# A transformer block with routed experts: experts' rows added by accumulating scatters, every shared chunk ahead of the experts

## The reference

```python
mod = (silu(c) @ wmod).reshape(4, 6, 1, 512)            # sa, ca, ga, sb, cb, gb per batch
ga, gb = sign(ga) * max(|ga|, 0.25), sign(gb) * max(|gb|, 0.25)
h = layernorm(x) * (1 + ca) + sa
x = x + ga * attention(h)        # 16 heads of 32, relu(q), relu(k); vk = [v;1] k^T per head and batch
                                 # out = vk q, divided by its last row, then @ w_proj.T + b_proj
h = layernorm(x) * (1 + cb) + sb
gate = top-2 of 8 experts by sigmoid(h @ gate_w.T) + router_bias, weights normalized
y = sum over the two experts e of gate_e * (silu(h W1[e]) * (h W3[e])) W2[e]     # 352 wide
s = (silu(h sw1) * (h sw3)) sw2                                                  # shared, 704 wide
out = x + gb * (y + s)
```

## Time and profile before

| what | us |
|---|---|
| three runs | 1329.02, 1335.45, 1338.58 (median 1335.45) |
| the profiled execution's own time | 1328.03 |
| its span | 1326.3 |
| PE busy in the span | 1229.3 (93%) |
| DVE, ACT, POOL busy | 664.9, 413.8, 396.9 |
| mean granted clock | 0.976 |

### The profile page before, as it was taken

The page is one execution under the profiler, slowest core; times in us unless marked ns, Lnnn a source line. Parts: engine busy times, 40 slices in busy tenths (PEclk is TensorE's granted clock), DMA queues, the critical chain, the costliest instruction groups (busy, mean ns, idle before and its releaser), DMA issues.

```text
span 1326.3 us, 25206 instructions
## 1 busy us (share of the span) xinstructions
PE 1229.3 (93%) x9054; PEld 781.5 (59%) x9054; DVE 664.9 (50%) x1382; ACT 413.8 (31%) x869; POOL 396.9 (30%) x367
## 2 busy tenths in 40 slices
PE   6998998998997998977896999999999999989998
PEld 2645665665565665654564565656656665657675
DVE  6455877867777666577884211111111111126465
ACT  4332444433443332423333122222222222212121
POOL 2112656655654433200001011111111111056552
PEclk9998999999999999988998999999999999989999
DMA  7714687898896865733444455555565565489986
GB/s 233 210 42 128 165 192 191 197 219 167 206 214 162 235 184 166 233 124 112 139 146 129 112 130 133 142 123 141 135 129 137 128 141 130 111 224 239 253 232 173
DMA packets 269204, 219.08 MB, mean 165 GB/s; under 512 B 188496, under 2 KB 200784, under 8 KB 268572
## 3 DMA queue, kind: packets, MB, share of 16 engines
q1 hardware_dynamic: 239832, 155.31, 45.7%
q0 software_dynamic: 12848, 35.40, 12.0%
q10 hardware_dynamic: 16408, 26.77, 6.4%
HBM read 116.69 MB, written 56.94 MB: 131 GB/s over the span
## 4 chain that ended last, share of the span: by engine, by line
PE 51%; DVE 15%; POOL 10%; DMA 10%; issue 8%; ACT 3%; SPq 2%; ACTq 1%; DVEq 0%; POOLq 0%
PE ps_o L86 6%; PE ps_o L88 6%; PE ps_o L87 6%; PE ps_vs L86 5%; PE ps_vs L87 5%; PE ps_vs L88 5%; DMA xt<-g 3%; DMA wp_raw<-in_wproj_t 2%; PE ps_vh L86 2%; PE ps_vh L88 2%; PE ps_vh L87 2%; POOL ol L412 2%; DVE w_all L682 2%; POOL h L388 2%; POOL h L399 2%
## 5 line engine op out<-in xcount | busy, mean ns | idle before, releaser
L471 POOL DMA_INDIRECT g<-h_d,slot_token x71 | 67.8, 956 | 507.1 <-DMA xt<-g 350.0
L86 PE MATMUL ps_o<-w_all,xt 128*128 x568 | 178.7, 315 | 11.6 <-DMA xt<-g 11.6
L88 PE MATMUL ps_o<-w_all,xt 128*128 x568 | 178.6, 315 | 0.0
L87 PE MATMUL ps_o<-w_all,xt 128*128 x568 | 178.6, 314 | 0.0
L914 DVE TENSOR_TENSOR at<-ps_y,at 128x384 f16<-128x384 f32 x71 | 39.6, 558 | 176.5 <-ACT at L1171 176.5
L909 DVE SCALAR_TENSOR_TENSOR a<-ps_o,a 128x352 f32<-128x352 f32 x71 | 37.3, 525 | 173.1 <-PE ps_o L88 173.1
L1176 ACT ACTIVATE y<-ps_vs,slot_weight 128x512 f32<-128x512 f32 x71 | 48.8, 688 | 230.6 <-PE ps_vs L88 230.6
L86 PE MATMUL ps_qh<-ht,wqkv 128*128 128x128 f16 x512 | 88.9, 221 | 8.3 <-DVE qt L549 4.9
L88 PE MATMUL ps_qh<-ht,wqkv 128*128 128x128 f16 x512 | 88.9, 221 | 0.0
L87 PE MATMUL ps_qh<-ht,wqkv 128*128 128x128 f16 x512 | 88.9, 221 | 0.0
L86 PE MATMUL ps_kh<-s_ht,sh 128*128 128x256 f16 x256 | 71.3, 278 | 12.4 <-DMA s_ht<-h2t_d 8.9
(11 more groups left out here) (240 smaller groups left out, 3179.6 us busy)
## 6 DMA issues: line engine op xcount, KB each, us to landing
y_d<-y SPq DMA_DIRECT2D x71, 256.0 KB, 3.5
w_stage<-in_w_d ACTq DMA_DIRECT2D x64, 176.0 KB, 2.5
xb<-in_x SPq DMA_DIRECT2D x32, 256.0 KB, 3.5
xr<-in_x SPq DMA_DIRECT2D x32, 256.0 KB, 3.7
x_d<-x SPq DMA_DIRECT2D x32, 256.0 KB, 3.4
h_d<-hl SPq DMA_DIRECT2D x32, 256.0 KB, 2.6
h2t_d<-h2t SPq DMA_DIRECT2D x32, 256.0 KB, 3.4
s_xs<-x_d SPq DMA_DIRECT2D x32, 256.0 KB
```

The lines of the kernel that those rows point to most:

```text
L86: nc.tensor.matmul(out, lh, rh, start=first, stop=False, skip_group_check=True)
L87: nc.tensor.matmul(out, lh, rl, start=False, stop=False, skip_group_check=True)
L88: return nc.tensor.matmul(out, ll, rh, start=False, stop=last, skip_group_check=True)
L471: pool.indirect_dma_start(m.g[:, t % 2, :], None, m.h2_d, bass.IndirectOffsetOnAxis(ap=m.slot_token[:, t:t + 1], axis=0)).then_inc(m.gathe ...
```

## The change

Diff, cut to its core:

```diff
-LAG = BT
+LAG = BT + 1
-EARLY = 9
-EARLY_STEPS = SH_TILES * EARLY
+EARLY_STEPS = SH_TILES * CHUNKS
-X_RING, QT_RING, ... Y_RING, YB = 4, 9, 3, 2, 3, 3, 6, 4, 4, 8
+X_RING, QT_RING, ... W_RING = 4, 10, 3, 2, 3, 3, 6, 4
+G_RING, GB_RING, Y_RING = 4, 3, 3
-TURNS_PER_STEP = 2
-TURNS_FROM = TAIL_STEPS + 7
+TURNS_FROM = TAIL_STEPS + 11
-LAST_PIECES = 4
+LAST_PIECES = 6
 def w_turn(q):
     if q < TAIL_STEPS:
-        return range(q, q + 1)
-    if q <= LIST_STEP:
-        return spread(TAIL_STEPS, SHARED_PIECES, q - TAIL_STEPS, LIST_STEP + 1 - TAIL_STEPS)
+        return range(q // 2, q // 2 + 1) if q % 2 else range(0)
     if q < EARLY_STEPS - LAST_PIECES:
-        return spread(SHARED_PIECES, E * WP, q - LIST_STEP - 1, ...)
+        return spread(TAIL_PIECES, E * WP, q - TAIL_STEPS, EARLY_STEPS - LAST_PIECES - TAIL_STEPS)
...
# POOL, the experts' stage: all 71 gathers, then fetch and fetch_onto of y_d, become
+    def gather_gate(t):
+        if t < SLOT_TILES:
+            r = t % GB_RING
+            at_least(pool, m.ey_ready, t - GB_RING + 1)
+            pool.indirect_dma_start(m.gbr[r][:, :], None, m.gb_d,
+                                    bass.IndirectOffsetOnAxis(ap=m.slot_batch[:, t:t + 1], axis=0)).then_inc(m.gbr_loaded[r], 16)
+    def scatter(t):
+        pool.wait_ge(m.ey_ready, t + 1)
+        at_least(pool, m.scattered, 16 * t)
+        pool.indirect_dma_start(m.out, bass.IndirectOffsetOnAxis(ap=m.slot_row[:, t:t + 1], axis=0), m.y[:, t % Y_RING, :], None,
+                                compute_op=ALU.add).then_inc(m.scattered, 16)
...
     for t in range(SLOT_TILES):
-        gather(t)
+        scatter(t)
+        gather(t + G_RING)
+        gather_gate(t + GB_RING)
+    pool.wait_ge(m.scattered, 16 * SLOT_TILES)
...
# DVE, after each e_multiply(t); ACT's e_out is gone, and SP's store_y too
+    def e_out(t):
+        r = t % GB_RING
+        v.wait_ge(m.ey_done, t + 1)
+        v.wait_ge(m.gbr_loaded[r], ring_use(t, GB_RING))
+        at_least(v, m.scattered, 16 * (t - Y_RING + 1))
+        v.scalar_tensor_tensor(out=m.y[:, t % Y_RING, :], in0=m.ps_ey[:, 0:C], scalar=m.slot_weight[:, t:t + 1], in1=m.gbr[r][:, :],
+                               op0=ALU.mult, op1=ALU.mult).then_inc(m.ey_ready, 1)
...
# PE: the modulation's four later rows, in slots 3 and 4
+    def modulate_turned():
+        for row, j in ((GA, 2), (GB, 5), (SHIFT, 3), (GAIN, 4)):
+            for c in range(KC):
+                for k in range(KC):
+                    at = j * C + c * P
+                    mm = nc.tensor.matmul(m.ps_modt[:, row, :, c], m.wmod[:, k, at:at + P], m.sct[:, k, :], start=k == 0, stop=k == KC - 1)
...
# PE, down(n): the last of the six inner parts of both tiles comes after the first five of both
-            j = SH_TILES - 1
-            if u == 0:
-                pe.wait_ge(m.at_lo, SH_TILES * n + j + 1)
+        j = SH_TILES - 1
+        pe.wait_ge(m.at_lo, SH_TILES * n + j + 1)
+        for u in range(2):
...
# PE, slots: from slot 32 on project_out(t - 1) stands behind the second shared step
-        project_out(t - 1)
+        if s < TILES:
+            project_out(t - 1)
...
# SP, slot 31: load_h(0) stands ahead of the slot's stores, loads and turns
+        if s == TILES - 1:
+            sp.wait_ge(m.ht_loaded[(TILES - 1) % HT_RING], ring_use(TILES - 1, HT_RING))
+            load_h(0)
         store_x2(t - 2)
...
# DVE: a batch's sums leave PSUM by 4 wide operations instead of 8, after centre(s + 2);
# the high half is now made by ACT (vk_high), the low half later in the slot (vk_low)
```

More of the change, by code:

```diff
@@ L114, in w_turn @@
     if q < TAIL_STEPS:
-        return range(q, q + 1)
-    if q <= LIST_STEP:
-        return spread(TAIL_STEPS, SHARED_PIECES, q - TAIL_STEPS, LIST_STEP + 1 - TAIL_STEPS)
+        return range(q // 2, q // 2 + 1) if q % 2 else range(0)
     if q < EARLY_STEPS - LAST_PIECES:
-        return spread(SHARED_PIECES, E * WP, q - LIST_STEP - 1, EARLY_STEPS - LAST_PIECES - LIST_STEP - 1)
+        return spread(TAIL_PIECES, E * WP, q - TAIL_STEPS, EARLY_STEPS - LAST_PIECES - TAIL_STEPS)
     return range(0)
 def down_due(q):
-    return q >= SH_TILES and q % SH_TILES == 0 and q // SH_TILES != EARLY
+    return q >= SH_TILES and q % SH_TILES == 0
 def add_due(q):
-    return q >= SH_TILES and q % SH_TILES == 1 and q // SH_TILES != EARLY
+    return q >= SH_TILES and q % SH_TILES == 1
 def list_turn(q):
-    first = TURNS_PER_STEP * (q - TURNS_FROM)
-    return range(first, first + TURNS_PER_STEP) if 0 <= first < TILES else range(0)
+    return range(q - TURNS_FROM, q - TURNS_FROM + 1) if tile(q - TURNS_FROM) else range(0)
 def step_width(j):
     return P if j < SH_TILES - 1 else SH_HALF
[L140 to L153, removed]
 def sync_program(nc, m, sp):
@@ L492, in fetch_onto @@
-    def fetch_onto(i):
-        r = i % YB
-        pool.wait_ge(m.y_loaded[i % Y_RING], 2 * ring_use(i, Y_RING) - 16)
-        pool.indirect_dma_start(m.yb[:, r, 0, :], None, m.y_d,
-                                bass.IndirectOffsetOnAxis(ap=m.slot[:, 1, order[i]:order[i] + 1], axis=0),
-                                compute_op=ALU.add).then_inc(m.y_loaded[i % Y_RING], 16)
-    for i in range(3):
-        fetch(i)
-    for i in range(len(order)):
-        fetch_onto(i)
-        fetch(i + 3)
+    gather(0)
@@ new lines, in gpsimd_program @@
+    gather(1)
+    pool.wait_ge(m.s_t1_done, 3 * BT)
+    gather_gate(0)
+    pool.wait_ge(m.at_lo, EARLY_STEPS)
+    gather(2)
+    gather(3)
+    gather_gate(1)
+    pool.wait_ge(m.s_xs_done, 2 * CHUNKS)
+    gather_gate(2)
+    pool.wait_ge(m.spare_stored, 16)
+    for j in range(2):
+        pool.wait_ge(m.s_xs_stored[j], 16 * CHUNKS)
+    for t in range(SLOT_TILES):
+        scatter(t)
+        gather(t + G_RING)
+        gather_gate(t + GB_RING)
+    pool.wait_ge(m.scattered, 16 * SLOT_TILES)
@@ L769, in vector_program @@
         if s >= TILES:
[L770 to L777 removed]
+            for p in (*w_turn(q), *w_turn(q + 1)):
                 w_low(p)
@@ L1105, in scalar_program @@
             split_high(n)
+            if s == -1 and n < 9:
+                load_stage(n + 3)
         if s == -2:
@@ L1424, in tensor_program @@
     e_up(0)
-    down(EARLY - 1)
+    down(CHUNKS - 1)
     pe.wait_ge(m.a_padded, 1)
@@ L1585, in place_buffers @@
     m.passed = sb("passed", [1, SLOT_TILES, E], F32)
-    sb = region(W_STAGE_AT, W_AT)
-    m.g = sb("g", [P, 2, 2 * C], F16)
-    m.xt = sb("xt", [P, 2, 2 * KC, P], F16)
+    GATE_AT, ACT_AT, AT_AT, T1_AT = SHARED_AT + 8192, SHARED_AT + 12288, SHARED_AT + 14336, SHARED_AT + 24576
+    first, second, third = region(W_STAGE_AT, W_AT), region(SHARED_AT + 4096, GATE_AT), region(SHARED_AT, SHARED_AT + 4096)
+    m.g = [(first, first, second, second)[j](f"g{j}", [P, 2 * C], F16) for j in range(G_RING)]
+    m.xt = [(first, first, third, third)[j](f"xt{j}", [P, 2 * KC, P], F16) for j in range(G_RING)]
+    m.gbr = [region(at, at + 2048)(f"gbr{j}", [P, C], F32) for j, at in enumerate((GATE_AT, ACT_AT, T1_AT))]
+    m.y = region(AT_AT, AT_AT + 6144)("y", [P, Y_RING, C], F32)
     sb = region(W_END, END)
```

401 lines of the change are left out of this document (154 added, 247 removed).

## The result

The changed kernel takes 1375.85 us (median of 4 runs, 1365.56 to 1379.96), the kernel before 1334.88 beside it: a ratio of 1.03, 95% interval 1.0228 to 1.0371. The forecast was 1307 us in a range of 1278 to 1365, so the time lies 69 us above the forecast and 11 above the range. The profiled execution has a span of 1377.2 us, and the gap is looked for there.

A forecast was written before the change was run, and what follows sets the result against it. PE was taken to set the pace, busy 1229.3 of 1326.3 us with 97 us idle. Terms -10 -7 -7 -20 -6 +6 -5 -3 +4 +3 +17 gave -28, a span of 1298, plus 9 for the median: 1307 us, range 1278 to 1365.

The forecast's parts named there:

- point 1: First shared chunk's load goes ahead of slot 31's turns, so its 8.9 us wait goes: -10 us (bounds -4 to -11).
- point 2: Slots up to 31: attention a slot later gives a batch's PSUM sums time to be ready: -7 us (0 to -11).
- Points 3 to 5: Shared chunks: fewer waits from slot 32 and in 541 to 717, clock gains, last stage gone: -7 -20 -6 +6 -5 -3 us.
- Point 6: Modulation: 13.9 us of PE removed, 128 narrow instructions at 140 ns, 17.9 us, added: +4 us (bounds -1 to +42).
- My own sign for it: Profile check in slot 3: PE's long group lasting over 20 us would show the modulation estimate wrong.
- Point 7: The end: a DVE operation, a scatter's issue of 1.6 us and its landing: +3 us (0 to +12).
- Point 8: Experts: chained scatters at 6.1 us a tile against PE's 5.87, +17 us (0 to +165); queues fit, barely.
- The term for the turned rows: Experts: scatter issue, gather landing, turn and queueing take 11.2 us, against the 11 or so PE needs; both loops at PE's pace.
- The rival of the scatter chain: Experts: each scatter waiting for the one before sets the pace, 6.5 us or more a tile; 1363 us at 6.9; chance 0.25.
- the rival of moved waits: Shared steps: DVE is late with something else, a third instead of most of points 2 to 5 comes; 1335 us; chance 0.13.

The follow-up runs named there:

- The edit of one step: Slot list's one-column mask products fed two steps behind VectorE's comparisons, not one, against the changed kernel with gather ahead and old modulation: 1308.64 us.
- two chains alone: Changed kernel with odd tiles' rows scattered into a second tensor, each scatter waiting only for the one two tiles back: 1378.65 us (one run).

## Why the prediction was wrong

**Points 1 and 2 (first load, slots).** The size came out, and half of it by luck. With the old modulation the first shared product comes at 413.7 us, 18.4 earlier than before, where I had 17. PE idles 10.7 us less up to there (27.5 for 38.2), and 8.9 of this is the load of the first chunk, as in point 1. It is busy 7.7 us less, and that is not point 2: with `LAG` at 9 one tile's attention, projection and logits, 32 products and 3.7 us in all, stand behind the first shared product instead of ahead of it, and the clock stood at half for 20 us up to there before and for none in this trace (10 and 7 us in the two others with the old modulation). The waits between batches, which point 2 priced at -7, moved to `v_sb`: PE idles 9.4 us in slots 12 to 31 for 11.0, and 8.1 in slots 2 to 11 for 7.0. The point had this step wrong. (Its stretch from 160 us begins in slot 11, not 14.)

**Points 3 to 5 (shared chunks).** Forecast -35, measured -23, and -22 to -27 over the nine kernels. I took three quarters of 27.5 us of idle time in one sum without asking which wait goes. The clock gained what I said (0.94 to 0.98), the waits for `s_at` went, and the masks' 10 us stayed to a tenth. A tile's masks are made on DVE one step before their products, as before; that there is one tile a step in place of two changed nothing. The edit of one step shows that the distance, not DVE's load, decides. And a term is missing from the sum: the new wait of 6.4 us for the logits. With it most of the 8.9 us of point 1 came back, one stage later, together with a clock at half.

**Point 6 (modulation).** Failed. I took 128 x 140 ns = 17.9 us. Their own cost at full clock is even less, 15.6. What I had no row for was a stretch of nothing but four-column products: the clock fell to 1.2 GHz 4 us into it, and the group took 23.6 us. With what followed it cost 14 us more than the old modulation up to the first shared product (means of six and of three traces) instead of 4. My own sign for it ("over 20 us") was met. The upper bound of +42 held it, the value taken did not.

**Point 7 (the end).** +6 for +3, inside its bounds: PE's last `e_down` is followed by the scale, a scatter's issue and its landing.

**Point 8 (the experts), the step that failed.** The chain of scatters was priced well: I took 6.1 us a tile from an accumulation on the chip, and once it decides, the scatters stand 6.34 apart with a landing of 5.5. The term for the turned rows behind the scatter was mis-sized. It set "11.2 us, against the 11 or so that PE needs" and let both loops "sit at PE's pace". The second number was right: 10.9 us are free at PE's pace. The first is 1.93 + 5.42 + 5.94 = 13.3 us in the changed kernel. I had taken the transfers at their landings of before (3.8 and 4.3 us) with 1.5 of queueing in all, and with an adding scatter in the same queue they take 5.4 and 4.9; with plain scatters the same order needs 8.3 us and the loss is gone. The excess also does not stay alone: from a tile's first product to its scatter it is 14.6 us instead of 12.6, by PE's wait for the tile between (0.8), the scatter's wait behind a finished `y` (0.6 more) and the clock. So the experts cost 68 us where the sum had 17 from the chain of scatters and nothing from the loop.

"PE's waits would then be 0.2 us each, too short for the clock" failed as well. PE waited for `xt` 33 times, 0.5 to 3.3 us each, and the clock stood at half for 34 us. PE was busy 445.0 us for products that take 423.9 at a clock of 1.00: of these 21 us, 15 are clock.

**The Trainium skill's rule** (DMA: Bandwidth & Descriptors, "Anatomy of one DMA — SWDGE (gpsimd) path"), that the receipt of a write is the long part of a DMA's fixed cost and longest where the target is HBM, is not borne out here: a plain scatter into memory lands in 3.2 us, a plain gather out of it in 3.4. An adding scatter into the same tensor takes 5.3 to 5.5 us, less than the 5.9 to 6.0, counted to its reader, of the accumulations on the chip that the sum was built on.

**The rival of the scatter chain** gave 1363 us, the value nearest the result, by a mechanism that two chains alone disproved as the only limit. The experts' stretch falls from 498 us (mean of three) to 461 with the gather ahead (mean of three), 443.6 with two chains added and 427.6 with scatters that do not add: steps of 37, 17 and 16 us, the last two from single runs; 427.6 is under the 434.8 of before. Open is whether an adding scatter is long by its packets of one row or by something else that adding needs; no run here separates them. Two slips of the sums do not matter: 0.23 x 71 is 16, not 17, and a third of 48 is 16, which would put the rival of moved waits at 1339 us, not 1335.

## What to carry to other kernels

When an engine issues prefetches and results from one in-order stream, sum the loop from a result through the prefetch behind it and back, in the durations that the new traffic will give, and divide by the depth of the ring; then put the prefetch ahead of the result. The sum is only as good as its landings: here the 1.5 us taken for the queues should have been 3.6 by the 13.3 measured. A limit that shows no gain when removed alone may be the next one: remove the first with it before calling it free. When a small group of products is moved or split, look at the granted clock of the stretch behind it as well as at the group's own length: here 8 us less in the group gained nothing.

## What the runs showed of the hardware

- An indirect scatter that adds takes POOL 1.62 us to issue and lands after 5.2 to 5.6 us (medians of six kernels); without the addition 0.99 and 3.2 us, for the same 256 KB. In the adding one each packet holds one row of 2048 bytes, in the plain one two.
- Other transfers beside an adding scatter are slower too: gather 5.4 us for 3.4 and turn 4.9 for 3.4 in the same order of issue, turn 6.0 with the gather ahead.
- 128 products of 128 x 128 weights and 4 columns in full precision, back to back, ran from 4 us after their start at half the granted clock, with PE never idle. In four parts of 4.5 and 3.7 us they took 122 ns each in the mean, 115 at full clock, and at or behind each part the clock stood at half for 3.4 to 6.8 us.
